# Eight of 41 closing tiles on GpSimd, and a three-to-one split of the stores, in a patch-embedding, fast-weight and mixture-of-experts block

## The reference

```python
h = tok(x, ln_gamma, ln_beta, W, b)              # shifted patches, layer norm, projection
h = concatenate([h, txt], axis=1)                # (32, 164, 192)
h = h + attn(layernorm(h), w_key, w_value, w_query, w_gate, w_out)   # fast-weight scan
# ffn(x), with x = layernorm(h): rms norm xf, router, top 2 of 8 experts
probs = softmax(xf @ router_w.T)
comb_w = probs * sel                             # sel marks the two largest per token
hid = silu(xf @ gate_w.T) * (xf @ up_w.T)        # per expert
y = einsum('tef,edf->td', hid * comb_w[:, :, None], down_w)
h = h + (y + x)                                  # the output
```

## Time and profile before

| | |
|---|---|
| median of 3 runs | 549.48 us (548.49 to 550.42) |
| span of the profiled execution | 547.2 us; the page gives no other time for this execution |
| instructions | 12568 |
| busy in the span | PE 484.7, PEld 461.4, DVE 375.3, ACT 304.8, POOL 192.3 us |
| bytes moved by DMA | 71.67 MB, mean 131 GB/s |

### The profile page before, as it was taken

How to read it: one execution, slowest core, us unless ns; L and a number is a source line. 1 busy time by engine, 2 the same in 40 slices (tenths; PEclk the granted TensorE clock), 3 DMA queues, 4 the chain that set the end, 5 groups by cost and what they waited for, 6 DMA issues and landing times.

```text
span 547.2 us, 12568 instructions
## 1 busy us (share of the span) xinstructions
PE 484.7 (89%) x3157; PEld 461.4 (84%) x3158; DVE 375.3 (69%) x1293; ACT 304.8 (56%) x773; POOL 192.3 (35%) x272
## 2 busy tenths in 40 slices
PE   2999998998798987789999999999999999999900
PEld 2999997887576876789999999999999999999800
DVE  4969996459789879848566566565565565565597
ACT  5485967449578876435444444444444444444473
POOL 1000000006577777733333333333433433433330
PEclk9999999999799989799999999999999999999965
DMA  8988214711433342542222222222222222235897
GB/s 322 415 331 350 63 53 130 283 38 51 120 94 110 101 126 76 139 117 73 71 76 76 68 79 73 68 82 70 68 83 69 69 83 68 68 84 145 273 353 223
DMA packets 62463, 71.67 MB, mean 131 GB/s; under 512 B 19057, under 2 KB 56626, under 8 KB 61410
## 3 DMA queue, kind: packets, MB, share of 16 engines
q1 hardware_dynamic: 49920, 51.43, 30.6%
q0 software_dynamic: 8208, 16.95, 8.7%
q10 hardware_dynamic: 4306, 2.95, 1.8%
HBM read 49.43 MB, written 21.86 MB: 130 GB/s over the span
## 4 chain that ended last, share of the span: by engine, by line
PE 71%; DVE 15%; DMA 6%; ACT 4%; issue 2%; ACTq 1%; SPq 0%; POOL 0%; DVEq 0%; POOLq 0%
PE bank L838 8%; PE pair L838 6%; PE bank L1088 5%; PE bank L1084 5%; PE bank L1087 5%; PE bank L1086 5%; PE bank L1085 5%; PE bank L1095 5%; PE pair L1104 4%; PE bank L1104 4%; PE pair L1073 3%; PE pair L983 3%; ACT yall L749 2%; PE pair L987 2%; PE pair L1106 2%
## 5 line engine op out<-in xcount | busy, mean ns | idle before, releaser
L782 POOL DMA_INDIRECT disp<-xf,posu x82 | 85.0, 1037 | 151.0 <-ACT xf L654 123.8
L1575 DVE TENSOR_TENSOR hh<-sg,bank 128x384 f32<-128x384 f32 x89 | 49.3, 554 | 99.5 <-ACT sg L730 99.5
L812 POOL DMA_INDIRECT ydram<-ysb,dnow x89 | 88.5, 994 | 69.4 <-DMA ydram<-ysb,dnow 35.1
L730 ACT ACTIVATE sg<-bank 128x384 f32<-128x384 f32 x89 | 43.7, 492 | 116.8 <-PE bank L1088 116.8
L1084 PE MATMUL bank<-wa,xh 128*128 x178 | 67.5, 379 | 0.0
L1088 PE MATMUL bank<-wa,xl 128*128 x178 | 60.4, 339 | 0.0
L1087 PE MATMUL bank<-wa,xh 128*128 x178 | 59.9, 337 | 0.0
L1085 PE MATMUL bank<-wa,xh 128*128 x178 | 59.7, 336 | 0.0
L1086 PE MATMUL bank<-wa,xl 128*128 x178 | 59.7, 335 | 0.0
L809 POOL COPY dnow<-dest 128x1 uint32 (+1 forms) x89 | 16.9, 190 | 114.2 <-DVE ysb L1585 104.8
L838 PE MATMUL bank<-wcT,imgT 128*128 128x193 f32 x240 | 41.7, 335 | 10.6 <-DMA imgT<-in_pixels 10.6
(11 more groups left out here) (262 smaller groups left out, 1171.2 us busy)
## 6 DMA issues: line engine op xcount, KB each, us to landing
xs<-disp SPq DMA_DIRECT2D x89, 96.0 KB, 2.0
band<-in_bands SPq DMA_DIRECT2D x4, 1536.0 KB, 12.1
yall<-ydram SPq DMA_DIRECT2D x7, 768.0 KB, 7.8
imgT<-in_pixels SPq DMA_DIRECT2D x4, 768.0 KB, 12.5
imgT<-in_pixels SPq DMA_DIRECT2D x2, 1536.0 KB, 16.0
hres<-in_text SPq DMA_DIRECT2D x1, 3072.0 KB, 25.5
wa<-in_gate_up_w SPq DMA_DIRECT2D x8, 384.0 KB, 8.5
ring<-in_gate_up_w SPq DMA_DIRECT2D x32, 96.0 KB
```

The lines of the kernel that those rows point to most:

```text
L782: pool.indirect_dma_start(disp, bass.IndirectOffsetOnAxis(ap=posu[c % XBUF][:, 2 * j + k:2 * j + k + 1], axis=0), xfd[c % XBUF][:, j, :], None
L812: pool.indirect_dma_start(ydram, bass.IndirectOffsetOnAxis(ap=dnow[b][:], axis=0), ysb[r][:], None).then_inc(s_ys[b], 16)
```

## The change

- VectorE no longer handles tiles 32 to 39 (groups 32 and 36). It does its nine other groups in the order 0, 4, ..., 28, 40. Tile 40's k = 0 row waits for the last lower load explicitly, since the tile that used to wait for it is no longer VectorE's.
- GpSimd, behind its last indirect DMA, takes groups 32 and 36: for each, four `tensor_scalar` (k = 0 row times weight, in place), one `tensor_tensor` adding the four tiles to `hres`, and, once `s_scaled` has reached the group's end, a second `tensor_tensor` adding the scaled k = 1 rows. It waits for its own semaphore between dependent steps. Each finished group counts `s_pfin` up.
- Stores go in the order 0, 4, ..., 28, 40, 32, 36. SyncE issues q = 0, 1, 2 of each group and ScalarE q = 3. ScalarE issues groups 0 to 24 between its tiles, and 28, 40, 32 and 36 after its last tile.

```diff
+POOLED = (32, 36)
+STORED = (*(t for t in range(0, TILES, GROUP) if t not in POOLED), *POOLED)
+SIDES = ((0, 1, 2), (3,))
...
         def store_group(eng, side, t):
             n = min(GROUP, TILES - t)
-            eng.wait_ge(s_fin, t + n)
-            for q in (2 * side, 2 * side + 1):
+            if t in POOLED:
+                eng.wait_ge(s_pfin, POOLED.index(t) + 1)
+            else:
+                eng.wait_ge(s_fin, t + n - GROUP * sum(p < t for p in POOLED))
+            for q in SIDES[side]:
                 eng.dma_start(out_q[q][:, t:t + n, :], hres3[32 * q:32 * q + 32, t:t + n, :]).then_inc(s_out[side], 16)
...
-            for t in range(0, TILES, GROUP):
+            for t in STORED:
                 store_group(sp, 0, t)
             for side in range(2):
-                sp.wait_ge(s_out[side], 16 * 2 * -(-TILES // GROUP))
+                sp.wait_ge(s_out[side], 16 * len(SIDES[side]) * -(-TILES // GROUP))
...
-                if n >= 2 * GROUP and n % GROUP == GROUP - 1:
+                if 2 * GROUP <= n < POOLED[0] + GROUP and n % GROUP == GROUP - 1:
                     store_group(act, 1, n + 1 - 3 * GROUP)
-            for t in range(TILES // GROUP * GROUP - 2 * GROUP, TILES, GROUP):
+            for t in STORED[POOLED[0] // GROUP - 2 + 1:]:
                 store_group(act, 1, t)
...
+            pool.wait_ge(s_upd, TILES)
+            pool.wait_ge(s_wts, 1)
+            for i, t in enumerate(POOLED):
+                for n in range(t, t + GROUP):
+                    if n in LOWER:
+                        pool.wait_ge(s_yl[LOWER.index(n)], 32)
+                    pool.tensor_scalar(yall4[:, 0, n, :], yall4[:, 0, n, :], wts[:, 2 * n:2 * n + 1], None, ALU.mult
+                                       ).then_inc(s_pool_low, 1)
+                pool.wait_ge(s_pool_low, (GROUP + 1) * i + GROUP)
+                pool.tensor_tensor(hres3[:, t:t + GROUP, :], hres3[:, t:t + GROUP, :], yall4[:, 0, t:t + GROUP, :], ALU.add
+                                   ).then_inc(s_pool_low, 1)
+                pool.wait_ge(s_pool_low, (GROUP + 1) * (i + 1))
+                pool.wait_ge(s_scaled, t + GROUP)
+                pool.tensor_tensor(hres3[:, t:t + GROUP, :], hres3[:, t:t + GROUP, :], yall4[:, 1, t:t + GROUP, :], ALU.add
+                                   ).then_inc(s_pfin, 1)
...
             lower(0)
-            for t in range(0, TILES, GROUP):
-                a, b = t, min(t + GROUP, TILES)
+            own = STORED[:-len(POOLED)]
+            for i, a in enumerate(own):
+                b = min(a + GROUP, TILES)
                 st.wait()
-                if b < TILES:
-                    lower(b)
+                if i + 1 < len(own):
+                    lower(own[i + 1])
                 v.wait_ge(s_scaled, b)
                 v.tensor_tensor(hres3[:, a:b, :], hres3[:, a:b, :], yall4[:, 1, a:b, :], ALU.add).then_inc(s_fin, b - a)
```

More of the change, by code:

```diff
@@ L328, in build @@
         s_yg = [sem(f"results_in{i}") for i in range(len(LOADS) - 1)]
+        s_pool_low, s_pfin = sem("pool_lower_added"), sem("pool_final_ready")
         s_fin, s_wts, s_scaled, s_out = sem("final_ready"), sem("softmax_ready"), sem("results_scaled"), [sem("out_stored_sp"), sem("out_stored_act")]
@@ L1595, in lower @@
                 for n in range(t, min(t + GROUP, TILES)):
-                    if n in LOWER:
-                        v.wait_ge(s_yl[LOWER.index(n)], 32)
+                    if n in LOWER or n == POOLED[-1] + GROUP:
+                        v.wait_ge(s_yl[sum(a <= n for a in LOWER) - 1], 32)
                     ins = v.scalar_tensor_tensor(out=hres3[:, n, :], in0=yall4[:, 0, n, :], scalar=wts[:, 2 * n:2 * n + 1],
```

## The result

The changed kernel takes 560.41 us (median of 4 runs, 559.32 to 561.31), the kernel before 548.99 in the same session (547.87 to 550.42, 4 runs). The ratio is 1.0207, 95% interval 1.019 to 1.0224: 11.4 us slower. Forecast were 554.6 us and a range of 549.0 to 557.5. The direction was right and the size was not: the time lies above the range.

The account below looks back on a forecast made before the run. VectorE's last sums and the stores behind them were taken to bound the end. GpSimd's chain ending at 548.5 plus 3.85 of stores gave a span of 552.35, 5.15 more; 549.48 + 5.15 = 554.6 us, range 549.0 to 557.5.

Parts of the forecast that it names:

- Stores: After GpSimd's last group: SyncE's three stores, the last 0.95 us later, then 2.9 us to the end, 3.85 us in total.
- The signs named beforehand: Profile signs: stretched VectorE instructions, its last sum 3 us or more after 539.9, GpSimd sums 1.2 to 2.3 us, GpSimd last.
- neither sign of being wrong: Forecast wrong if GpSimd's second group ends before 543, or if VectorE, not GpSimd, releases the last stores.
- case A: Closing stage: GpSimd and VectorE lock each other out both ways, VectorE losing 3.0 us; 552.0 to 557.5 us, chance 0.58.
- The sum, taken as 1.7: GpSimd's 128 x 768 two-input add: 1.7 us, about the middle of bounds 1.2 and 2.3.
- The product, taken as 0.32: GpSimd's 128 x 192 `tensor_scalar`: 0.32 us, bounds 0.25 from a memset and 0.38 from an affine_select.
- From tile 35's scaling to GpSimd's end: GpSimd's closing chain, from 540.1 to 548.5: waits, three sums, four products, turns with VectorE's last three instructions.
- ScalarE's and SyncE's new split: SyncE's three stores a group take 1.3 us of a 2.19 us pace, so cost nothing; ScalarE waits for VectorE anyway.
- held for the whole instruction: Shared SBUF port: all GpSimd time charged to VectorE while both work, 3.0 us for the first group.
- B: Rival: GpSimd waits for VectorE, VectorE for nobody; span +1.0 us, 550.5 us, chance 0.15.
- C: Rival: no contention to speak of for streaming operands; span +0.55 us, 550.0 us, chance 0.15.
- D: Rival: GpSimd adds as fast as VectorE, 0.9 us, neither holding the other; span -2.15 us, 547.3 us, chance 0.12.

Follow-up runs that it names:

- experiment 1: Changed kernel with GpSimd's drain at the end of the program left out: 554.69 us, ratio 1.0093 to the kernel before.
- experiment 2: Kernel before with a wait for VectorE's last sum and a one-element memset added at the end of GpSimd's list: 555.37 us, ratio 1.0104.
- experiment 5: Kernel before with the late one-element GpSimd memset, plus an explicit GpSimd drain behind its last indirect DMA: 549.13 us, ratio 1.0019.
- experiment 9: Changed kernel with an explicit GpSimd drain between the scatters and the slots' stores: 557.74 us, ratio 1.0155 to the kernel before.
- experiment 3: Kernel before with stores split three to one between SyncE and ScalarE, nothing on GpSimd: 549.26 us, ratio 0.9999.
- experiment 7: Changed kernel without the end drain, GpSimd's twelve arithmetic instructions replaced by memsets of the same outputs: 548.04 us, ratio 0.999 to the kernel before.
- experiment 12: Changed kernel without the end drain, with group 32 alone on GpSimd: 553.04 us, ratio 1.0078 to the kernel before.
- experiment 6: Changed kernel without the end drain, GpSimd's twelve instructions set behind VectorE's last sum so the two never overlap: 558.98 us, ratio 1.019.

## Why the prediction was wrong

The step that failed is the one under *Stores*: "2.9 us later all is over". It took the stores, 3.85 us in all, as the only thing behind the last work, and put GpSimd's drain at nothing by not naming it. The drain ended 9.2 us after that engine's last instruction and 6 us after the stores, so that 558.8 - 549.41 = 9.4 us lay behind the last sum, not 3.85. Experiments 1, 2 and 5 show it by taking it away, by causing it alone, and by hiding it again. In the kernel before GpSimd ended at 529.46 and the drain had 8.5 us to spare. The change moved GpSimd's end by 20 us. The question that wasn't asked is what an engine has to do after its last instruction, and the row that answers it was in the trace.

The signs named beforehand don't catch this. VectorE's long products, sums of 1.80 us and a last group by GpSimd all appeared, VectorE's last sum ended at 542.81, 2.9 us behind 539.9, and neither sign of being wrong did: GpSimd's second group ended at 549.41, and GpSimd released the last stores. No sign looked behind the stores.

Without the drain the changed kernel takes 554.69 us, and 554.6 had been forecast. So close an agreement is partly luck, since terms cancel:

- *VectorE loses two groups, and is held up itself (case A).* Right in kind. Expected were 3.0 us for the first group, measured 2.24: GpSimd's four products, though 3.0 us long by themselves, cost VectorE 0.08 + 0.14 + 0.33 = 0.55, and the sum of 1.81 cost it 3.06 - 1.40 = 1.66. So a product holds VectorE for far less than its length and a sum for nearly all of it. Tile 35 was scaled at 538.00 + 1.49 = 539.5, not 540.1. ScalarE in the changed kernel:

```profile
538.00 1.49 ACT L756 ACTIVATE yall<-yall,wts 128x192 f32<-128x192 f32 x4 [2.36 <-DVE hres L1633]
```

- *The sum, taken as 1.7,* is 1.80 alone. The one that met VectorE's sum at 539.98 took 2.64, 0.84 more, about VectorE's 0.87: the wait that the rows of before showed on an indirect DMA. In experiment 9 the same meeting went the other way: GpSimd's sum started first, at 539.32, and took 1.80, and VectorE's product of 539.34 took 1.99 instead of 0.41.
- *The product, taken as 0.32 with 0.38 as the high bound,* is 0.75 (2.99 / 4). This term was mis-sized by more than its bounds. The affine_select of 128 elements was a poor neighbour, and the trace of before had no arithmetic on this engine that was nearer. The tail had 1.28 us for four and 1.55 for VectorE's turns among them, 2.83 together. In fact VectorE had only its small last sum left (it ended at 542.81, the products began at 542.58) and the four took 3.08: two errors that cancel.
- *From tile 35's scaling to GpSimd's end* 8.4 us were expected, and 9.9 measured (539.5 to 549.41): 0.3 more up to the first sum's start, 0.94 in that sum (2.64 for 1.7), 0.25 in the products and 0.2 in the last two sums, less 0.15 in the gaps.
- *Behind the last group* 3.85 us were expected for the stores. Without the drain it is 553.0 - (547.74 + 1.80) = 3.5.
- *ScalarE's and SyncE's new split costs nothing in the pace:* right within some 1 us (experiment 3), but only while groups end 2.19 us apart. Experiments 7 and 12 show SyncE's queue as the next bound, as the text had said for "a pace under 1.3".

Of the rivals, B and C fall with VectorE's stretched products and experiment 6, and D with the sum's 1.80 us. Contention that both sides feel, and only with reads, is also what the Trainium skill states (SBUF — State Buffer, section "Who interferes with whom"): GpSimd's memsets left VectorE's group 24 at 15.87 us, its reading instructions put it at 18.10. A lock "held for the whole instruction", as the prediction took it, fits the sums but not the products, whose 3.0 us cost VectorE 0.55. Why is open.

## What to carry to other kernels

Before giving work to an engine that has been idle at the end, look at what it does after its last instruction: an end that was hidden may become the kernel's end. Where GpSimd has issued indirect DMAs, put an explicit drain in a stretch in which it idles anyway, so that the last one is short. And where two engines hold each other up, work moved from one to the other can cost more than it frees: one group moved freed 2.19 us of VectorE and cost it 3.76 (experiment 12). The next bound has to be looked at too, here the queue that issues the stores.

## What was not expected of the hardware

GpSimd's drain took 0.18 us where no indirect DMA had been issued, and 0.082 us more for each one since the last drain (40, 82 and 89 DMAs: 3.47, 6.90 and 7.48 us), data landed or not; with 171 it took 9.3 us. A second drain with none in between took 0.18. A GpSimd `tensor_scalar` with a weight per partition took 0.75 us for 192 elements, the `tensor_tensor` 1.80 for 768. A GpSimd product of 0.75 us held VectorE's two-operand instructions by some 0.14 us on average, a sum of 1.80 by 1.55 to 1.66, and GpSimd's memsets, which read nothing, by nothing.
